# Own staging for the second position set, and half of the last local group's maxima in main0

## The reference

```python
# layer 0: global attention with decomposed relative position terms
qkv = gn(x) @ w_qkv.T + b_qkv
rel_h = einsum('bhwc,hkc->bhwk', r_q, Rh)
rel_w = einsum('bhwc,wkc->bhwk', r_q, Rw)
scores = q @ k.T * SCALE + (rel_h[..., :, None] + rel_w[..., None, :])
x = x + (softmax(scores) @ v) @ w_proj.T + b_proj
# layer 1: 7 x 7 neighbourhood attention plus 16 register keys
scores = where(mask_cat, q1 @ concat(k1, reg_k).T / 4, -1e30)
x = x + (softmax(scores) @ concat(v1, reg_v)) @ out_w.T + out_b
```

## Time and profile before

| what | value |
|---|---|
| median of 3 runs | 4899.63 us (4899.4 to 4906.94) |
| the profiled execution | 4902.5 us |
| its span on the core | 4900.8 us |
| mean granted clock of TensorE | 0.951 |
| TensorE matmul busy | 4491.2 us (92%) |
| VectorE busy | 3079.3 us (63%) |
| ScalarE busy | 2608.5 us (53%) |

### The profile page before, as it was taken

The page is one execution under the profiler, slowest core; times in us unless marked ns, Lnnn a source line. Parts: engine busy times, 40 slices in busy tenths (PEclk is TensorE's granted clock), DMA queues, the critical chain, the costliest instruction groups (busy, mean ns, idle before and its releaser), DMA issues.

```text
span 4900.8 us, 97559 instructions
## 1 busy us (share of the span) xinstructions
PE 4491.2 (92%) x32598; PEld 2291.5 (47%) x32598; DVE 3079.3 (63%) x5558; ACT 2608.5 (53%) x3955; POOL 892.5 (18%) x1901
## 2 busy tenths in 40 slices
PE   5879999999999999999999999999999999999998
PEld 3334453544535454453544535455454544535444
DVE  3736667665675656667566675656657566676654
ACT  1533556555564555556555564555646555565564
POOL 3112111222202212121212202212021121102111
PEclk7888999999999999999999999999999999999999
DMA  6334242443414433253433424433144432424401
GB/s 126 83 73 86 49 104 62 99 90 70 89 39 106 87 87 71 53 108 70 99 79 70 88 52 99 94 73 84 44 106 81 99 79 48 101 62 99 87 14 40
DMA packets 235869, 386.05 MB, mean 79 GB/s; under 512 B 58396, under 2 KB 133728, under 8 KB 235360
## 3 DMA queue, kind: packets, MB, share of 16 engines
q1 hardware_dynamic: 189280, 266.13, 23.8%
q10 hardware_dynamic: 21504, 75.51, 7.6%
q0 software_dynamic: 24576, 37.80, 4.8%
HBM read 227.79 MB, written 88.08 MB: 64 GB/s over the span
## 4 chain that ended last, share of the span: by engine, by line
PE 75%; DVE 9%; SPq 5%; issue 5%; DMA 5%; ACT 2%; DVEq 0%; ACTq 0%; POOL 0%
PE P L1135 15%; PE P L1153 14%; PE P L1094 13%; PE P L958 6%; PE P L959 6%; DVE mx L901 5%; PE P L1071 5%; PE P L1185 4%; PE P L1206 4%; PE P L1102 3%; DMA QA<-queries 2%; PE P L1178 1%; SPq L507 1%; DMA biases<-xn 1%; DVE mxc L907 1%
## 5 line engine op out<-in xcount | busy, mean ns | idle before, releaser
L901 DVE TENSOR_REDUCE mx<-P 128x1 f32<-128x512 f32 x3072 | 1923.2, 682 | 471.2 <-PE P L1094 467.9
L771 ACT ACTIVATE probs<-P 128x1024 f32<-128x1024 f32 x1536 | 1507.5, 1022 | 777.7 <-PE P L1153 777.0
L1094 PE MATMUL P<-K,AR 96*128 96x256 f16 x6144 | 1093.1, 282 | 42.9 <-DMA AR<-biases 26.7
L1153 PE MATMUL P<-AR,K 113*128 113x512 f16 x3072 | 924.8, 383 | 14.1 <-DMA AR<-mrow 13.6
L907 DVE TENSOR_REDUCE mxc<-P 128x1 f32<-128x336 f32 (+1 forms) x1536 | 648.2, 474 | 307.6 <-PE P L1103 304.0
L787 ACT ACTIVATE probs<-P 128x320 f32<-128x320 f32 (+3 forms) x1632 | 618.1, 436 | 405.2 <-PE P L1206 340.0
L1135 PE MATMUL P<-probs,V 128*17 128x512 f32 x6144 | 817.2, 604 | 9.9 <-ACT probs L771 9.9
L1094 PEld LDWEIGHTS P<-K,AR 96*128 96x128 f16 x6144 | 541.7, 99 | 566.9 <-DVE mx L901 198.3
L1153 PEld LDWEIGHTS P<-AR,K 113*128 113x128 f16 x3072 | 216.9, 98 | 676.6 <-ACT probs L771 517.8
L1206 PE MATMUL P<-A,K 113*128 113x320 f16 (+2 forms) x1536 | 447.1, 306 | 12.9 <-ACT probs L787 12.1
L1102 PE MATMUL P<-K,A 112*128 112x320 f16 (+1 forms) x1536 | 400.4, 295 | 53.4 <-DVE mx L901 35.8
(11 more groups left out here) (122 smaller groups left out, 3705.4 us busy)
## 6 DMA issues: line engine op xcount, KB each, us to landing
AR<-biases SPq DMA_DIRECT2D x384, 256.0 KB, 7.7
AR<-queries ACTq DMA_DIRECT2D x96, 512.0 KB, 5.8
biases<-xn SPq DMA_DIRECT2D x192, 256.0 KB, 2.9
AR<-queries ACTq DMA_DIRECT2D x96, 256.0 KB, 8.5
K<-oraw POOLq DMA_DIRECT2D x384, 64.0 KB, 4.8
xin<-in_x_dram SPq DMA_DIRECT2D x16, 768.0 KB, 10.5
queries<-oraw SPq DMA_DIRECT2D x384, 32.0 KB, 4.8
QA<-queries SPq DMA_DIRECT2D x192, 64.0 KB, 5.1
```

Of the source, the lines that this page charges most:

```text
L771: nc.scalar.activation(probs[:, u % RING, j:j + 2, :], P[:, b:b + 2, :], ACT.Exp).then_inc(p_done[0], 1)
L901: V_.reduce_max(mx[:, n // 2, n % 2:n % 2 + 1], bank, AX.X).then_inc(used, 1)
L1094: last = mm(bank[:, QD * (v % 2):QD * (v % 2) + QD], AR[0:ROWS_MAX[0], part % SLOTS, v, c, j, 128 * q:128 * q + 128], K0[0:ROWS_MAX[0], h, ...
L1153: last = mm(P[:, j, :], K0[0:ROWS, h, 128 * kt:128 * kt + 128], AR[0:ROWS, p % SLOTS, kt // 2, :, j, :], start=True, stop=True)
```

## The change

- The staging of group 1's position terms gets its own place: xin seen as f16 and a new tile `rest`. relhi and rello become lists by group. A set of group 1 no longer waits for another set; that of group 2 waits for group 0's, as does the ones row that GpSimd writes to xn. rcp gives up its space and lies in QA's second slot.
- The queries of group 1 are loaded to QA at the end of `operands_out`, behind all query writes, and no longer behind fill 0.
- The set of group 1 moves in main1 from steps 24 to 27 to steps 8, 10, 12, 14; ask 1 and fill 1 move from step 6 to 28, ask 2 and fill 2 from 28 to 45.
- The set of group 2 moves in main0 from steps 8 to 11 to 8, 11, 14, 17.
- 16 of the 33 local maximum jobs of group 2 move from main1 to main0: there they stand with the 33 of group 1, spread over steps 73 to 94, where group 1's alone had steps 77 to 93. The other 17 stay in steps 0 to 24 of main1.

```diff
+THIRD = 16
-    placed += [(8 + n, job) for n, job in enumerate(rel_jobs(image, 2))]
+    placed += [(8 + 3 * n, job) for n, job in enumerate(rel_jobs(image, 2))]
-        placed += evenly(max_jobs(1, i1, 0), 13, 32) + evenly(max_jobs(1, i1, 1), 77, 94)
+        placed += evenly(max_jobs(1, i1, 0), 13, 32)
+        placed += evenly(max_jobs(1, i1, 1) + max_jobs(1, i1, 2)[:THIRD], 73, 95)
...
-        placed = evenly(max_jobs(1, image, 2), 34 if i0 is None else 5, 62)
+        placed = evenly(max_jobs(1, image, 2)[0 if i0 is None else THIRD:], 34 if i0 is None else 5, 62)
...
-    placed = evenly(max_jobs(1, image, 2), 0, 25)
+    placed = evenly(max_jobs(1, image, 2)[THIRD:], 0, 25)
-    placed += [(0, ask(n0, 0)), (5, fill(n0, 0)), (6, ask(n0, 1)), (6, fill(n0, 1))]
-    placed += [(24 + n, job) for n, job in enumerate(rel_jobs(n0, 1))]
-    placed += [(28, ask(n0, 2)), (28, fill(n0, 2))]
+    placed += [(0, ask(n0, 0)), (5, fill(n0, 0)), (28, ask(n0, 1)), (28, fill(n0, 1))]
+    placed += [(8 + 2 * n, job) for n, job in enumerate(rel_jobs(n0, 1))]
+    placed += [(45, ask(n0, 2)), (45, fill(n0, 2))]
...
-        relhi, rello = (xn[:, n, :].bitcast(F16).rearrange("p (k h q) -> p k h q", k=2, h=GH) for n in range(2))
+        rest = sb("rest", [128, GH * QD], F16)
+        spare = xin[:].rearrange("p t c -> p (t c)").bitcast(F16)
+        tables = [xn[:, n, :].bitcast(F16)[:, k * S:(k + 1) * S] for n in range(2) for k in range(2)]
+        others = [spare[:, k * S:(k + 1) * S] for k in range(3)] + [rest[:]]
+        relhi, rello = ([[t.rearrange("p (h q) -> p h q", h=GH) for t in (s[2 * n:2 * n + 2])]
+                         for s in (tables, others, tables)] for n in range(2))
-        rcp = sb("rcp", [128, 2, 4, NH])
+        rcp = QA[:, 1, 0, 0:16 * NH].bitcast(F32).rearrange("p (q t h) -> p q t h", q=2, t=4)
...
                         sp.dma_start(queries[g, s, :, :, j, :],
                                      t[D * j:D * j + D, g, :].rearrange("d (a n) -> d a n", a=4)
                                      ).then_inc(queries_out[g], 16)
+                query_blocks(im, 1)
...
-                    if part in (0, 2):
-                        query_blocks(image, part // 2 + 1)
+                    if part == 2:
+                        query_blocks(image, 2)
...
-                    g, image = (1, im) if again else (2, im) if L == 0 else (1, im + 2)
+                    g, image = (0, im) if again else (2, im) if L == 0 else (0, im + 2)
...
-                        if part:
-                            pe.wait_ge(biases_out[part - 1], (image + 1) * PER_BIASES)
+                        if part == 2:
+                            pe.wait_ge(biases_out[0], (image + 1) * PER_BIASES)
```

More of the change, by code:

```diff
@@ L387, in rel_view @@
             table, part = n // 2, 8 * (n % 2)
-            t = operand[:, table, :, :].rearrange("p h (l w) -> p h l w", w=16)
+            t = operand[table].rearrange("p h (l w) -> p h l w", w=16)
             if table == 0:
@@ L479, in biases_away @@
                         sp.dma_start(biases[g, table, :, s].rearrange("k a h n -> k a (h n)"),
-                                     t[:, table, :, :]).then_inc(biases_out[g], 16)
+                                     t[g][table]).then_inc(biases_out[g], 16)
             def fill_slot(im, p):
@@ L808, in high_parts @@
                         act.wait_ge(rel_done, consumed(job)[1])
-                        src, dst = rel_view(P[:, JOB_BANKS[L][at % JOBS], :], job[4], relhi)
+                        src, dst = rel_view(P[:, JOB_BANKS[L][at % JOBS], :], job[4], relhi[job[3]])
                         copy(dst, src).then_inc(relhi_done, 1)
@@ L886, in low_parts @@
                         dve.wait_ge(relhi_done, value)
-                        (src, high), (_, low) = rel_view(bank, n, relhi), rel_view(bank, n, rello)
+                        (src, high), (_, low) = rel_view(bank, n, relhi[part]), rel_view(bank, n, rello[part])
                         V_.tensor_tensor(low, src, high, ALU.subtract).then_inc(used, 1)
```

## The result

The changed kernel takes 4864.44 us (median of four runs, 4862.39 to 4868.74), the kernel before 4899.51 us beside it (4897.09 to 4906.94). The ratio is 0.9931, with a 95% interval of 0.9919 to 0.9943: faster by 0.7%, or 35 us. The forecast was 4893 us. The profiled execution has a span of 4860.6 us for 4900.8.

What follows compares the result with a forecast made beforehand. No single slow engine: TensorE busy 92%, leaving its half clock, waits and places paced by others. 81 - 22 - 66 - 1.5 = -8.5 us on 4902.5, by the median 4891, rounded up to 4893 us; range 4878 to 4908, over rivals 4858 to 4930.

Steps and rivals of the forecast that it cites:

- Part 1: End of main0: 16 local maxima moved in cost +3.5 us in steps 73 to 76, +1.9 after; +81 us in all.
- The rival that TensorE's order alone sets this price: End of main0 takes the maxima at +2.9 us instead of +5.4; total -46, 4854 us; chance 0.07.
- Part 2: Main0, group 2's set spread to steps 8, 11, 14, 17: -0.6 us and -0.85 for the clock; -22 us in all.
- Part 3: Main1, group 1's set moved to steps 8 to 14 with its own staging: -4.7 us a round, 14 times, -66 us.
- The landing of the queries, 15.7 us: Group 1's queries reach QA 15.7 us into main1 (15.2 to 16.5), so TensorE waits 3.6 us at step 8.
- a sign of being wrong: Main1, step 8: a QA wait under 2 us would show the prediction wrong; 3.6 us was forecast.
- The half clock, 2.9 us: Main1: clock falls after the query wait; long fall 0.45 of rounds, short 0.45, none 0.1; costs 2.9 us a round.
- The fall of 13.6 us: Main1: half clock lasting through all four position jobs, costing 4.5 to 5 us; as every-round rival 4927 us, chance 0.28.
- the nearest rival: Main1: the clock comes back at once, moving group 1's set gives -6.5 to -7.6 us; 4858 us, chance 0.25.
- What cost nothing: Main1 and next main0: later fills 1 and 2 are free; fill 0 lands at 26.2 us, 2 us before its reader.

Runs made afterwards that it cites:

- e3: The changed kernel with the 49 local maxima of main0 spread from step 77 instead of 73: 4859.96 us, ratio 0.9926 to the kernel before.
- e9: The changed kernel with group 1's set at steps 12 to 18 of main1 and only 8 maxima moved, spread from step 77: 4850.52 us, ratio 0.9907.
- e1: The kernel before with only the 16 local maxima moved to the end of main0: 4972.93 us, ratio 1.0155.
- e2: The changed kernel with no local maxima moved, group 1's at steps 77 to 93 as before: 4879.73 us, ratio 0.9969 to the kernel before.
- e7: The changed kernel with ask 1 and fill 1 back at step 6 of main1 instead of 28: 4935.09 us, ratio 1.0064 to the kernel before.
- e11: The changed kernel with group 1's set at steps 12 to 18 of main1 and no maxima moved: 4867.96 us, ratio 0.9947 to the kernel before.
- e8: The changed kernel with group 1's set at steps 12, 14, 16, 18 of main1 instead of 8, 10, 12, 14: 4834.12 us, ratio 0.9863.
- the shared staging: The changed kernel with all three position sets staged in xn again, the wait for the first set's writes back: 4925.1 us, ratio 1.0043.

## Why the prediction was right in direction and wrong in size

The forecast was a gain of 7 us, less than the measurement can tell from none, with a chance of 0.43 for faster; 35 us were measured. That the sign was right is owed to the net of three sums, two of which held; the third was off by more than the whole forecast, and toward faster.

**Part 1** was right. Forecast +3.5 and +1.9, measured +3.9 and +1.8; the sum +5.7 against +5.4 lies inside the bounds given. The job by job reckoning with three banks held to half a microsecond, and VectorE, whose 8.8 us it put ahead, is busy for 8.66 of the 10.8 us of steps 73 to 76. (In e3, and for main1 in e9, the same reckoning was too low by 0.8 us a round and more, so its closeness here is in part luck.) The rival that TensorE's order alone sets this price (+2.9) is out. e1 and e2 show the same prices for these two stages, whatever main1 does: in main0 the parts do add up.

**Part 2** was nearly right. Where the clock stays up the stage takes 27.0 us, 0.5 below the 27.5 of the earlier trace rows (forecast 0.6). But the clock still falls in 5 of 14 rounds, and such rounds take 28.4 to 30.1 us. The forecast had most of the clock's cost going away; half of it did.

**Part 3** is the step that failed, by size: -8.4 for -4.7. The mechanism, an old wait at a new place, was right. In absolute times the forecast said 35.1 us for steps 0 to 31, and 31.2 were measured. Two terms of its sum carry the 3.9 us:

- *The landing of the queries, 15.7 us.* Measured 14.0. The moment of issue was nearly right: 11.0 us forecast (1791.0 + 8.8 is 1799.8, so 11.2 by the rows), 10.4 to 11.3 measured. The landing time was not: I took the heavier moments of the earlier trace rows for a guide, 2.4 us and more behind the issue and 4.7 us from first issue to last landing, and it came in 3.3. That is 1.7 us, and it moves everything after it. TensorE also came to the job sooner than at the forecast's 12.1 us, at 9.9 to 12.3, so the wait was 2.5 us on average for 3.6, and in six rounds under the 2 us that the prediction had named as a sign of being wrong. The Trainium skill (DMA: Bandwidth & Descriptors, section Anatomy of one DMA) puts a transfer on the path over GpSimd at a fixed 2.0 us or so and its bytes at 436 GB/s; for 64 KB that makes an estimate of 2.15 us by this page. The 2.0 us measured here on SP's queue agree, in a moment with little beside them; e7's 7.2 us do not.
- *The half clock, 2.9 us.* At the landing that was measured, the full-clock sum is 32.2 - 1.7 = 30.5 us. The measured mean is 31.2, so by this estimate the half clock costs 0.7 us, not 2.9. The fall of 13.6 us, to which I gave 0.45 of the rounds, does not occur in any. Each round has 3.4 to 6.8 us at half clock, so the clock doesn't simply come back, as the nearest rival had it; its fall is short. In the seven rounds where it falls only inside steps 0 to 7 it costs nothing visible: TensorE is slower on its way to a load for which it would have waited anyway, and step 32 comes at 30.2 to 30.6 us. In the other seven it falls (in one of them for the second time) at the end of the wait or behind it, over the short and the first long job, and step 32 comes at 31.7 to 32.5: a late fall costs some 1.7 us, the difference of the two means (32.1 and 30.3). By the Trainium skill (TensorE: Matmul & The Clock Gate, section Terms) half of the throttled time would be lost, 3.1 of these 6.3 us. The trace shows about a quarter of that, for the reason just told.

What the forecast didn't see is how its parts depend on each other. It priced the sixteen maxima in main1 at 0.18 us of TensorE each (0.9 for five of them). That price is right where no second set stands beside them: in e1, steps 0 to 23 without the sixteen take 19.5 us for 22.6, or 0.19 us each. Beside the second set e2 and e11 show 7.1 and 7.2 us for sixteen, 0.45 us each, the clock included. The forecast's terms for main1 took them as already gone. With the sixteen put back at that price in 14 rounds (+40), parts 2 and 3 alone would come to -22 - 66 + 40 = -48 us; e2 measured -15, although part 3 as a whole turned out better than its term. Part 1 alone cost 78 us, and together they give -35: the parts are worth some 98 us more together than apart. Two things make this up. In the kernel before, the time that the maxima free in main1 goes into the wait for the queries (e1: 0.9 us a round is left). Beside the second set, their going shortens TensorE's waits for VectorE, which must wait for ScalarE's copy, and the half clock. The waits are in the trace of e11, about 1 us of the 7; why the clock stays low for longer is not shown.

**What cost nothing** held in the changed kernel. No wait for AR<-biases shows at step 25; fill 0 lands at 23.8 to 24.6 us, 26.2 was forecast. That the late fill is more than harmless was missed: e7 prices ask 1 and fill 1 at 5.1 us a round (1.3%). The forecast counted what the load would wait for on SP, and not what would travel beside it.

**Open.** Three things. The rounds divide by whether the clock falls again or only behind the wait: seven with such a late fall and seven without in the changed kernel, one and thirteen in e8, all with the same instructions in steps 0 to 7. I found nothing in the records that decides it. In e11 the clock stays down longer behind the second set when maxima lie between the jobs, although TensorE counts as busy for 17.56 of the 19.7 us; which of its instructions let the clock fall was not tried. And the new place of the query load on SP, ahead of the first set's writes and fill 0, was not undone by itself, so its share of part 3 has no price of its own.

## What to carry to other kernels

Where work is moved out of a stage to make room for something else, price it in the company that it leaves: the sixteen maxima cost 0.19 us each in the kernel before, up to the next wait, 0.36 where they went, and would have cost 0.45 beside the position jobs that came in. A move that loses 1.55% alone was part of a gain of 0.7%, so test the parts of such a change together and also one at a time. When a wait remains after a change, look at what arrives when. Here the fixed point was the landing at 14 us, and moving the reader four steps later was worth another 0.7%. Look also at what travels beside a transfer on the critical path: ask 1 and fill 1 at their old place cost 5.1 us a round, as much as the shared staging (4.8).

## What the runs showed of the hardware that was not expected

- Four loads of 64 KB took 2.0 us each to land in the changed kernel, 2.4 to 3.6 us in the moment of the earlier trace rows, and up to 7.2 us in the round of e7 shown, where 0.75 MB were asked for in their midst; there only the loads that were issued behind that request were slow (5.4 and 7.2 for 1.9 and 2.5 us).
- The clock fell with TensorE mostly busy and without a long wait: in the changed kernel 5.5 to 7 us into main1 in eight rounds, during or behind the long jobs of the first set, and in five rounds of main0 behind the first long job of the third. In the first row below, from the start of main1 to the fall, TensorE is busy for 5.44 of 6.30 us, and its longest wait is 0.60 us; the second row is the stretch at half clock:

```profile
1778.70:1785.00 6.30, 5.44 (x76) 4.49 (x76) 3.13 (x6) 3.98 (x10) 6.03 (x13) 1.00 1.07 188
1785.00:1791.80 6.80, 6.49 (x24) 3.34 (x22) 2.58 (x5) 2.14 (x6) 6.18 (x12) 0.50 0.71 112
```

- The long position jobs took the same time at both levels of the clock, 2.05 us at the full and 2.07 at the half; the short ones took 0.63 and 1.02 us (medians of the changed kernel). Both are 16 matmuls of 64 columns; in the long ones the elements of the moving operand lie 16 apart.
- A half clock can be free. Of 6.3 us a round only some 0.7 showed in the time, as in half of the rounds the fall lay ahead of a wait.
